# A six-layer perceiver stack on one core: an earlier norm, a maximum ahead of rounding, and two VectorE programs without loops

## The reference, cut to what matters

```python
# layer 1 (adapter attention), for each layernormed row; the adapter is a context of 257 rows for each sequence
q = split_heads(hidden_states @ Wq, q_len);  k = split_heads(hidden_states @ Wk, q_len)
v = split_heads(hidden_states @ Wv, q_len)
q = q * cos + _rotate_half(q) * sin;         k = k * cos + _rotate_half(k) * sin
...
a_k = split_heads(adapter @ Wk, adapter_len)
a_v = split_heads(adapter @ Wv, adapter_len)
a_scores = jnp.tanh(gate) * softmax(...)
```

## Time and profile before

| | |
|---|---|
| runs | 2551.22, 2546.84, 2542.56 us; median 2546.84 |
| the profiled execution | 2551.28 us, its span 2549.1 us |
| busy: PE, DVE, ACT, POOL | 2021.6, 1869.5, 1400.2, 474.1 us |
| layer 1's projections | 28.55 to 154.70 us |
| layer 4 | about 1263 to 1840 us |
| layer 6 | about 2100 to 2542.4 us |

### The profile page before, as it was taken

The page is one execution under the profiler, slowest core; times in us unless marked ns, Lnnn a source line. Parts: engine busy times, 40 slices in busy tenths (PEclk is TensorE's granted clock), DMA queues, the critical chain, the costliest instruction groups (busy, mean ns, idle before and its releaser), DMA issues.

```text
span 2549.1 us, 51234 instructions
## 1 busy us (share of the span) xinstructions
PE 2021.6 (79%) x15447; PEld 1440.2 (56%) x15486; DVE 1869.5 (73%) x5158; ACT 1400.2 (55%) x3709; POOL 474.1 (19%) x561
## 2 busy tenths in 40 slices
PE   4689999999999688565799999999866756665655
PEld 4667777777776555232566766667655543333332
DVE  3348888778787456798577787877457768888887
ACT  1035655555655243453366656666545647776775
POOL 0011122111121000010243343333134430000000
PEclk9999999999999799676899999999978777899998
DMA  2001111111110200200012112111010000000000
GB/s 97 0 15 30 30 32 29 29 29 29 30 32 16 80 1 1 92 1 34 13 47 63 55 50 63 54 38 30 18 28 11 10 8 1 0 0 0 0 0 33
DMA packets 64759, 71.83 MB, mean 28 GB/s; under 512 B 40402, under 2 KB 42131, under 8 KB 63636
## 3 DMA queue, kind: packets, MB, share of 16 engines
q1 hardware_dynamic: 64660, 70.73, 9.3%
HBM read 63.47 MB, written 2.10 MB: 26 GB/s over the span
## 4 chain that ended last, share of the span: by engine, by line
PE 58%; DVE 23%; issue 9%; ACT 8%; DVEq 1%; DMA 1%; SPq 0%; POOL 0%; ACTq 0%; POOLq 0%
PE ps L645 5%; PE ps L616 5%; PE ps L607 4%; PE ps L629 3%; PE ps L677 3%; PE ps L1831 3%; PE ps L1814 3%; PE ps L579 3%; PE ps L1771 2%; PE ps L1761 2%; PE ps L2194 2%; PE ps L1840 2%; DVE f_ams L2505 2%; PE ps L1796 2%; DVE d_ks L1613 2%
## 5 line engine op out<-in xcount | busy, mean ns | idle before, releaser
L362 ACT ACTIVATE a_pr<-ps,a_nm 128x257 f32<-128x257 f32 x512 | 238.1, 473 | 183.1 <-DVE a_nm L476 183.1
L1563 ACT ACTIVATE d_pr<-d_st,d_nm 128x257 f32<-128x257 f32 x256 | 128.2, 502 | 207.4 <-DVE d_nm L1683 197.8
L484 DVE COPY a_pT<-ps 128x512 f32<-128x512 f32 x256 | 170.3, 686 | 92.7 <-PE ps L645 92.1
L2578 PE MATMUL ps<-f_wt,f_nxT 128*128 128x512 bf16 x481 | 150.1, 436 | 68.4 <-DVE f_act L2489 63.1
L476 DVE TENSOR_REDUCE a_nm<-ps 128x2 f32<-128x514 f32 x256 | 174.4, 681 | 0.0
L645 PE MATMUL ps<-ident,a_pr 128*128 128x128 f32 x1024 | 160.4, 279 | 0.0
L1814 PE MATMUL ps<-d_kc,d_qc 128*128 128x257 f32 x512 | 147.2, 412 | 0.0
L645 PEld LDWEIGHTS ps<-ident,a_pr 128*128 128x128 f32 x1024 | 117.5, 141 | 33.4 <-issue 12.7
L607 PE MATMUL ps<-a_cT,a_wqk 128*128 128x257 f32 x512 | 133.2, 382 | 2.9 <-DVE a_k L450 1.7
L302 POOL TENSOR_TENSOR a_sf<-a_sf,a_ratio 128x256 f32<-128x256 f32 x64 | 39.4, 616 | 507.0 <-DVE a_ratio L505 507.0
L616 PE MATMUL ps<-a_wvg,a_cT 128*128 128x256 f32 x512 | 129.4, 396 | 0.0
(11 more groups left out here) (350 smaller groups left out, 5313.9 us busy)
## 6 DMA issues: line engine op xcount, KB each, us to landing
a_cT<-in_ctx SPq DMA_DIRECT2D x64, 257.0 KB, 2.7
d_cT<-in_ctx SPq DMA_DIRECT2D x64, 257.0 KB, 2.8
f_wf<-in_f_w SPq DMA_DIRECT2D x24, 512.0 KB, 3.7
a_vbd<-a_vself SPq DMA_DIRECT2D x256, 8.0 KB
e_vb<-e_vs SPq DMA_DIRECT2D x256, 8.5 KB
c_wf<-in_c_w SPq DMA_DIRECT2D x3, 1024.0 KB, 7.1
x_all<-in_x SPq DMA_DIRECT2D x1, 2048.0 KB, 8.0
d_wo<-in_d_wo SPq DMA_DIRECT2D x1, 2048.0 KB
```

What stands on the lines that cost most here:

```text
L362: ins = act.activation(pr[j][:, g, :], ps[:, S_BANK[u % 2] + k, S:LK], ACT.Exp, bias=nm[j][:, g:g + 1], accum_out=ssum[j][:, 0, g:g + 1])
L484: dve.tensor_copy(pT[u][:, :, :, :], ps[:, T_BANK[u % 2], :].rearrange("p (g c q) -> p g c q", g=2, c=2))\
L1563: ins = act.activation(pr[j][:, g, :], st[u][:, k, :], ACT.Exp, bias=nm[u][:, k:k + 1], accum_out=sm[j][:, g:g + 1])
L2578: ins = pe.matmul(ps[:, 2 + 2 * k + w, :], lhsT=nxT[s][:, c, :], rhs=wt[:, 3 * e + w, c * IE:c * IE + IE], start=(c == 0), stop=(c == KT - 1))
```

## The change

In layer 1, SP loads the gate, the value weight, the context's last rows and a mask first, counted by a semaphore of their own (`w_early`), and the rest of the weights behind them. DVE takes the statistics of the 16 tiles ahead of the gated value weight. PE and ACT wait for the early four alone, and PE waits for the rest ahead of the first queries and keys. In the tile loop DVE's norm of tile t+2 now stands ahead of the rotation of tile t. In layer 4, DVE's six turns are written out. In layer 6, DVE's fourteen looped tiles are written out; `sizes(u)` stands ahead of `clamp(u - 1)`; ACT does both gates of a pair in a row and rounds pair u-1 behind `turned_out(u - 2)`, where it rounded pair u-2 ahead of the first gate; PE does both up products in a row and turns behind them. DVE's program grows from 1729 to 3132 rows, those of PE, ACT, POOL and SP change by less than five.

```diff
-        w_loaded = shared("w_loaded", 16 * 10, 1)
+        w_early, w_loaded = shared("vb_loaded0", 16 * 4, 1), shared("w_loaded", 16 * 6, 1)
...
         def sp(eng):
-            for dst, name in ((wqk, "a_wqk"), (wv, "a_wv"), (wo, "a_wo"), (rope, "a_rope"), (hmask, "a_hmask"),
-                              (own, "a_own"), (tmask, "a_tmask"), (gate, "a_gate"), (ctail, "a_ctail"),
+            for dst, name in ((gate, "a_gate"), (wv, "a_wv"), (ctail, "a_ctail"), (tmask, "a_tmask")):
+                eng.dma_start(dst[:], d[name]).then_inc(w_early.sem, 16)
+            for dst, name in ((wqk, "a_wqk"), (rope, "a_rope"), (hmask, "a_hmask"), (own, "a_own"), (wo, "a_wo"),
                               (amask, "a_amask")):
                 eng.dma_start(dst[:], d[name]).then_inc(w_loaded.sem, 16)
...
         def vector(dve):
-            dve.wait_ge(w_loaded.sem, w_loaded.at(1, 0))
+            dve.wait_ge(x_loaded.sem, x_loaded.at(1, 0))
+            with dve.Fori(0, NT) as t:
+                finish_tile(dve, 0, t)
+            dve.wait_ge(w_early.sem, w_early.at(1, 0))
             dve.wait_ge(gate_ready.sem, gate_ready.at(0, 1))
             dve.tensor_tensor(wvg[:, :, :], wv[:, :, :], spread(tgate[:, :], 1, KT), ALU.mult)\
                 .then_inc(wvg_ready.sem, 1)
-            dve.wait_ge(x_loaded.sem, x_loaded.at(1, 0))
-            with dve.Fori(0, NT) as t:
-                finish_tile(dve, 0, t)
             norm_vector(dve, n)
...
-            rotate(0, 0)
+            dve.wait_ge(w_loaded.sem, w_loaded.at(1, 0))
             with dve.Fori(0, NT // 2 - 1) as i:
                 for j in range(2):
                     norm_out(i * 2 + (j + 2), j)
-                    rotate(i * 2 + (j + 1), 1 - j)
+                    rotate(i * 2 + j, j)
+            rotate(NT - 2, 0)
             rotate(NT - 1, 1)
...
             for j in range(2):
                 turn_x(j, j)
+            pe.wait_ge(w_loaded.sem, w_loaded.at(1, 0))
             queries_keys(0, 0, first=True)
...
-        def steps(eng, step):
+        def steps(eng, step, written_out=False):
...
-            with eng.Fori(0, (B - 4 * BT) // (2 * BT)) as i:
+            def turn(i):
                 for o in range(2 * BT):
                     step(i * 8 + (BT + o), (BT + o) % 8, i * 2 + (1 + o // BT), i * 4 + (BT + o + 1) // 2,
                          Hosted(i * 4 + o // 2, o // 2, i, o % 2 == 1))
+
+            turns = (B - 4 * BT) // (2 * BT)
+            if written_out:
+                for i in range(turns):
+                    turn(i)
+            else:
+                with eng.Fori(0, turns) as i:
+                    turn(i)
...
-            steps(dve, step)
+            steps(dve, step, written_out=True)
...
-        def tiles(eng, parts, step):
+        def tiles(eng, parts, step, written_out=False):
...
-            with eng.Fori(0, NT // 2 - 1) as i:
-                step(i * 2 + 1, 1, True)
-                step(i * 2 + 2, 0, True)
+            if written_out:
+                for t in range(1, NT - 1):
+                    step(t, t % 2, True)
+            else:
+                with eng.Fori(0, NT // 2 - 1) as i:
+                    step(i * 2 + 1, 1, True)
+                    step(i * 2 + 2, 0, True)
...
                 for u in range(PAIRS if more else PAIRS + LAG):
-                    if u - LAG < PAIRS:
-                        rounded_up(u - LAG)
                     gate(u, 0)
+                    gate(u, 1)
                     turned_out(u - LAG)
-                    gate(u, 1)
+                    if u - 1 < PAIRS:
+                        rounded_up(u - 1)
...
                     if u < PAIRS:
                         products(u)
+                        sizes(u)
                     clamp(u - 1)
-                    if u < PAIRS:
-                        sizes(u)
                     output(u - LAG)
...
-            tiles(dve, parts, step)
+            tiles(dve, parts, step, written_out=True)
...
                     up(u, 0)
+                    up(u, 1)
                     turn(u - LAG)
-                    up(u, 1)
```

More of the change, by code:

```diff
@@ L321, in scalar @@
         def scalar(act):
-            act.wait_ge(w_loaded.sem, w_loaded.at(1, 0))
+            act.wait_ge(w_early.sem, w_early.at(1, 0))
             act.activation(tgate[:, :], gate[:, :], ACT.Tanh).then_inc(gate_ready.sem, 1)
@@ L551, in tensor @@
         def tensor(pe):
-            pe.wait_ge(w_loaded.sem, w_loaded.at(1, 0))
+            pe.wait_ge(w_early.sem, w_early.at(1, 0))
             pe.wait_ge(const_loaded.sem, const_loaded.at(1, 0))
```

## The result

The changed kernel takes 2458.89 us (median of 4 runs, 2457.05 to 2462.12), the kernel before 2545.45 us beside it; the ratio is 0.9659, interval 0.9638 to 0.9679. That is 86.6 us less. The forecast was 2467 us, 80 less than 2546.84, range 2446 to 2489. The profiled executions are 91.3 us apart in span: that of before was a long one among its runs.

The account below looks back on a forecast made before the run. No engine bounds all: PE and DVE take turns in layer 1, PE bounds layer 4, DVE layer 6. -52 - 6 - 7 - 14 = -79, rounded -80: 2551.3 - 80 = 2471.3, less 4.4 is 2467 us; range 2446 to 2489.

Parts of the forecast that it names:

- Forecast 52: Layer 1's projections: 47.8 us less in the tile loop and 4.9 less at the start, together -52.
- The bound of -46: Layer 1: the smallest gain allowed for its term, if four more tiles run at the slow clock.
- The rival in which PE stays at the lower clock: Layer 1: L579 takes 5.36 instead of 3.74 us in all tiles, +23, so 2490 us; chance 0.07.
- Forecast 6: Layer 4 written out on DVE: register instructions and the branch back go, -6 us, bounds 0 to -32.
- 8 steps x 6 turns x 0.09 = 4.3 us: Layer 4: PE's wait for `d_ks` falls from 0.52 us in the loop to 0.43 written out.
- Forecast -7: Layer 6's order: the clamp's 17.3 us wait for ACT's rounding goes, lost overlap costs 10; bounds -17 to +10.
- 1.22 + 5 x 0.15 = 2 us more: Layer 6: time the clamp gains for ACT's rounding by standing behind the maximum and five small operations.
- The first rival: Layer 6: the wait moves to PE's down products or the next products, giving 2484 us; chance 0.13.
- The overlap: Layer 6: the maximum directly behind its products loses 0.16 us of overlap in 64 pairs, +10 us.
- Forecast -14: Layer 6 written out: DVE's idle time at register instructions goes, -14 us, bounds 0 to -14.
- forecast 21: Layer 6: order (-7) and writing out (-14) together, leaving the stage 421 us long.
- The last rival: Loading the longer DVE program stalls DVE and cancels the gain, 2550 us or more; chance 0.03.

Follow-up runs that it names:

- the two parts alone: Kernel before with only layer 1's norm put ahead of the rotation, 49.0 us less; and with only the early loads and statistics first, 4.8 us less.
- e4: Kernel before with layer 4's DVE loop kept as two turns, each of three old ones: 2538.71 us against 2546.09.
- e3: Kernel before with only layer 4's six DVE turns written out: 2535.89 us against 2546.09.
- e9: Kernel before with layer 6's new order on DVE and PE only, ACT as before, loops kept: 2569.6 us against 2545.89.
- e5: Kernel before with only layer 6's order changed, on DVE, ACT and PE, loops kept: 2532.75 us against 2547.27.
- e10: The changed kernel measured again: 2460.97 us against 2545.89 for the kernel before.
- e6: Kernel before with only layer 6's DVE program written out, old order kept: 2538.8 us against 2547.27.
- e7: Kernel before with layer 6's DVE loop as two turns of six tiles, two tiles written out: 2548.62 us against 2547.27.
- e12: Changed kernel with DVE's loops of layer 3, layer 5 and layer 1's sequences also written out: 2454.03 us against 2545.89 for the kernel before.
- e1: Kernel before with only layer 1's order of norm and rotation changed: 2497.07 us against 2546.09.

## Why the prediction was right

**Layer 1: right in mechanism and size.** Forecast 52, measured 49.0 + 4.8 = 53.8 by the two parts alone. The bound of -46 had tiles that stay at the lower clock; there are none. Part of the 2 us more is seen in the rows: the 15 intervals take 69.7 us where 70.4 were forecast, and the context product took 5.36 us where the sum had 6.12. The rival in which PE stays at the lower clock fell: PEclk went up with PE's busy share.

**Layer 4: right in size, and in cause as far as e4 shows; the working was thin.** Forecast 6, measured 7.3 from the turns without a slow stretch, 7.7 from the mean stages, and 10.2 (interval 7.6 to 16) by e3's median, which has some 4 us of clock in it. The stage of the changed kernel was 13.9 us shorter in its profiled execution; the rest is slow stretches, 8 against 5, whose number differs from kernel to kernel with no order that I found. The working, "8 steps x 6 turns x 0.09 = 4.3 us; other such places bring me to -6", rested on one row and a guess, and that it came out near is partly luck.

**Layer 6, the order: right in sign, the size off by a factor of two, and the reason given was incomplete.** Forecast -7, measured -14.5 (12 in the stage). The step that the clamp "has 1.22 + 5 x 0.15 = 2 us more" holds for the wait itself. But the prediction took ACT's edit for a risk with slack against it, and it is what makes the gain: DVE's move alone costs 31 us. The first rival foresaw that the wait could move to the products, and blamed the two gates ahead of the turned copy; in e9, where the copy stands between the gates, the products wait 36.2 us for the second gate, in e5, where it stands behind them, 2.9. The overlap was priced at +10; DVE's idle time in e5 is 431.0 - 385.3 = 45.7 us against 57.9, 12 less where 17.3 went, so the price was about 5. A likely reason: the clamp now stands between the last small operation and the addition to x, and covers the 0.09 us that DVE idled there.

**Layer 6, written out: the size too large alone.** Forecast -14, measured -8.5 alone; the clamp's wait grew by 5.8 us, which makes the difference. Together with the new order the stage lost 20 us (e10: 21.6), forecast 21. So the order's term, too small by 5 to 7 us, and this one, too large by about as much, made up for each other in the sum.

The Trainium skill's Advanced Engine Details and Errata, section Sequencer Loop, says that other engine instructions can be read and queued while a control instruction executes. Read as a promise that register work costs nothing, it is contradicted by the 8.5 us of e6 against nothing in e7, and by the 0.9 us a turn of layer 4; where long operations are queued it holds, as the 2.8 us behind layer 4's branch, covered but for 0.12 us in e4, show.

**The last rival, loading the longer program, fell.** Fewer instruction packets came, 54 against 63, and e12 shows no stall. Its premise that a loop stays loaded holds for layer 6's loop (276 instructions, no packet in a turn) and not for layer 4's (346, 5 packets in each). The Trainium skill's Runtime: NRT & Kernel Launch, section Instruction fetch mechanics, says that crossing a block is mostly hidden and that a taken branch out of the loaded pages stalls; the 2.8 us behind the branches of layer 4 and of e7 agree with the second, and e12's stage with the first.

## What to carry to other kernels

When an engine waits for a product that another engine makes late because of its own order, move it ahead of the work that waits for the first engine: two engines that took turns then overlap, for 48 us here. Before moving an operation on one engine, follow what its later result holds up in the queues of the next engines: the same move of the maximum cost 31 us alone and gave 14.5 with ACT's and PE's order changed too. Don't judge by busy shares where writing a loop out will pay: layer 3, where DVE is busy 154 of 175 us, gave 2 us, and layer 4, where PE is the busier engine, gave 7. Look instead for idle time of the engine behind its own results. When testing a loop with a longer body, look for a reload at its branch back: it cost e7 3.1 us at one branch, which the shorter loop did not have.

## What was not expected of the hardware

TensorE's granted clock rose as the engine got busier: 0.91 at a busy share of 70%, 1.00 at 98% in the same loop (0.98 in e1). In layer 4, at a busy share of 91%, short stretches at the lower level remain, each 1.25 to 1.4 us longer than the same work at the higher one (74.99 against 73.74 us a turn in e1), and 3 to 11 of them in one execution. They are part of why the runs of this kernel spread by 0.3%: among 21 runs of before, the slowest had a granted clock of 0.906 and the fastest 0.912. And whether a loop on DVE is loaded again at each turn went with its length: the one of 276 instructions and the shorter ones were not, those of 346, 820 (e7) and 1022 (e4) were, with 2.8 us behind the branch or more in which DVE got no instruction. So a program almost twice as long loaded fewer packets than the one with the loops.
